# An edge pass of a graph kernel: a new begin of the pass, group words read earlier, a sorted stretch evicted at an earlier column, and per-group bookkeeping on VectorE

## The reference

```
n = x.shape[0]
h = x @ Wn + bn
for l in range(4):
    Q = h @ WQ[l] + bQ[l];  K = h @ WK[l] + bK[l];  V = h @ WV[l] + bV[l]
    scores = jnp.sum(Q[dst] * K[src], axis=-1) * scale
    e = jnp.exp(scores - segment_max(scores, dst)[dst])
    attn = e / segment_sum(e, dst, n)[dst]
    messages = segment_sum(attn[:, None] * V[src], dst, n)
    h = layernorm(h + messages @ WO[l] + bO[l], ln_g[l], ln_b[l])
return h @ Wout + bout
```

## Time and profile before

| what | value |
|---|---|
| time, median of 3 runs | 7103.49 us (7101.05 to 7110.28) |
| the profiled execution's own time | 7094.96 us |
| its span | 7093.5 us |
| busy: PE, PE's weight loads, DVE, ACT, POOL | 66%, 54%, 61%, 37%, 66% of the span |
| granted TensorE clock, mean | 0.811 |
| attend passes | about 798 to 1619, 1744 to 2566, 2690 to 3509, 3629 to 4448 us |
| heads pass | about 4763 to 5780 us |

### The profile page before, as it was taken

The page is one execution under the profiler, slowest core; times in us unless marked ns, Lnnn a source line. Parts: engine busy times, 40 slices in busy tenths (PEclk is TensorE's granted clock), DMA queues, the critical chain, the costliest instruction groups (busy, mean ns, idle before and its releaser), DMA issues. The chain is left out here.

```text
span 7093.5 us, 128253 instructions
## 1 busy us (share of the span) xinstructions
PE 4693.2 (66%) x28386; PEld 3840.8 (54%) x28387; DVE 4300.3 (61%) x13524; ACT 2623.5 (37%) x7476; POOL 4669.2 (66%) x4886
## 2 busy tenths in 40 slices
PE   5420377775777775777667777445555555998999
PEld 4310266654565554665546655323333334997998
DVE  7550266663666654666556666447776765776665
ACT  0200244434444443444444443315555543554111
POOL 1367577774777765777667777337777755776777
PEclk9555688887888887888778888677777776998999
DMA  5310233332333313333233333123333324333332
GB/s 188 99 37 0 62 92 91 88 84 63 87 90 89 89 50 96 89 90 89 62 86 89 89 90 82 49 89 105 105 105 105 105 69 117 97 96 84 96 95 82
DMA packets 404728, 615.56 MB, mean 87 GB/s; under 512 B 213510, under 2 KB 256049, under 8 KB 403940
## 3 DMA queue, kind: packets, MB, share of 16 engines
q0 software_dynamic: 169952, 363.29, 19.0%
q1 hardware_dynamic: 211190, 200.20, 9.9%
q10 hardware_dynamic: 23122, 47.29, 2.0%
HBM read 528.33 MB, written 82.09 MB: 86 GB/s over the span
## 5 line engine op out<-in xcount | busy, mean ns | idle before, releaser
L1973 POOL DMA_INDIRECT rows<-table_d,meta x2432 | 2307.4, 949 | 887.5 <-issue 728.6
L2037 PE MATMUL ps_total<-weighted_rows,ident 128*128 128x129 f32 (+1 forms) x6464 | 1404.3, 374 | 596.8 <-ACT weighted_rows L2197 483.7
L2037 PEld LDWEIGHTS ps_total<-weighted_rows,ident 128*128 128x128 f32 x6464 | 1149.8, 226 | 857.0 <-issue 670.4
L2373 DVE SCALAR_TENSOR_TENSOR prod<-rows,q_rows 128x129 f32<-128x129 f32 x2432 | 690.0, 293 | 639.3 <-issue 391.1
L1973 POOL DMA_INDIRECT rows<-pairs_d,meta x800 | 773.7, 967 | 257.7 <-issue 243.4
L2073 PE MATMUL dense_sums<-x_rows,dense_power_t 128*128 128x129 f32 x3528 | 593.9, 320 | 460.8 <-DVE dense_rows L2264 443.2
L2073 PEld LDWEIGHTS dense_sums<-x_rows,dense_power_t 128*128 128x128 f32 x3528 | 534.0, 230 | 501.5 <-issue 501.5
L2141 ACT ACTIVATE weighted_rows<-rows,power 128x129 f32<-128x129 f32 x2432 | 729.4, 389 | 5.1
L2159 ACT COPY dense_power_t<-dense_turned 128x512 f32<-128x512 f32 x504 | 265.1, 526 | 1030.7 <-PE dense_turned L2064 1022.1
L2197 ACT ACTIVATE weighted_rows<-once_weighted,of_relation 128x136 f32<-128x136 f32 x1600 | 485.6, 393 | 193.6 <-DVE once_weighted L2433 190.3
L2254 DVE CUSTOM_DVE_ANT_0 dense_masked<-dense_scores,dense_masked,dense_least 128x896 f32<-128x896 f32 x252 | 289.2, 1148 | 413.0 <-PE dense_scores L2055 289.9
(11 more groups left out here) (704 smaller groups left out, 8908.3 us busy)
## 6 DMA issues: line engine op xcount, KB each, us to landing
dense_masked<-dense_masks_d SPq DMA_DIRECT2D x252, 448.0 KB
rows<-table_d,meta POOLq DMA_INDIRECT x2432, 2.5
dense_masks_d<-unmasked ACTq DMA_DIRECT2D x9, 3136.0 KB
src_store<-near_window_d SPq DMA_DIRECT2D x50, 384.0 KB, 3.8
near_window<-near_window_d SPq DMA_DIRECT2D x48, 384.0 KB, 3.6
rows<-pairs_d,meta POOLq DMA_INDIRECT x800, 2.8
tile_rows<-table_d,tile_halves POOLq DMA_INDIRECT x441, 2.6
tile_rows<-made_d,tile_halves POOLq DMA_INDIRECT x441, 2.6
```

The lines of the kernel that those rows point to most:

```text
L1973: pool.indirect_dma_start(rows[q][:, j, 0:width], None, table_d, bass.IndirectOffsetOnAxis(meta[q][:, j, number:number + 1], 0)).then_inc( ...
L2037: mm = pe.matmul(total[:, q, ds(part, 1), 0:W].rearrange("p a w -> p (a w)"), k.ident[:], wide[:, j % WS, :], start=False, stop=True, skip ...
L2373: own(dve.scalar_tensor_tensor(prod[:, j % 2, :], rows[q][:, j, :], -1.0, query, ALU.mult, ALU.mult, accum_out=score[:, j, :]))
```

## The change

1. **Begin of a pass.** The constants stand outside a block, so the engines no longer meet behind them. ACT issues the load of `x_rows` only after the first list has landed (`listed[0]`), in parts of 8 and 41 tiles. PE turns the first two groups of tiles, then makes the queries and unit 0's scores, and then turns the other eleven groups, in other banks. ACT copies in that order. The nine loads of the next weights go from ACT's queue to SP's, behind the whole pass.
2. **Words read ahead.** In a dense turn PE calls `load_words` for group 0 after the first unit of the part (u = 0, u = 4). The clearing of the bank moves to `add_columns`.
3. **Sort's stretch** is evicted at step 0 (column 1) instead of step 5 (column 11). The wait for `placed` moves there from step 2.
4. **DVE's semaphores** `own` and `sorted` are cleared at the begin of a group or a turn, and count from 0.
5. **`step_of`** divides and takes the remainder.

```diff
+            def x_ps(n):
+                return dense_ps[:, n] if n < 2 else (sum_ps, power_ps)[n % 2]
...
-            return (loaded[j // PAIRS] >> ((6 if j < PAIRS else 0) + 2 * (j % PAIRS))) & 3
-
-        with nc.Block() as block:
-            @block.vector
-            def _(dve):
...
+            return loaded[j // PAIRS] // ((64 if j < PAIRS else 1) * 4 ** (j % PAIRS)) % 4
+
+        def constants_of_pass(dve):
...
+        constants_of_pass(nc.vector)
...
                     turns(sp, body)
+                    if fetch is not None:
+                        fetch_layer(sp, m, k, *fetch)
...
                         pe.sem_inc(read[q], 1)
-
+                        return loaded
+
+                    def clear_sums(i, q):
                         pe.wait_ge(m["sum_taken"], i * 2 + (q + 1))
                         clear(q)
-                        return loaded
 
                     def add_columns(i, q, loaded, columns):
+                        if columns[0] == 0:
+                            clear_sums(i, q)
...
                                 if u in (0, 4):
                                     count_earlier(i)
+                                    loaded = load_words(i, 0)
                                 if u == 2:
-                                    add_columns(i, 0, load_words(i, 0), range(S))
+                                    add_columns(i, 0, loaded, range(S))
                                 if u == UNITS - 1:
-                                    loaded = load_words(i, 0)
                                     add_columns(i, 0, loaded, range(S // 2))
...
-                        for n in range(XGROUPS):
-                            if n == 0 or n == 6:
-                                pe.wait_ge(m[f"x_loaded{n // 6}"], 16)
-                            if n >= 2:
-                                pe.wait_ge(m["xt"], n - 1)
+                        def turn_x(n):
                             for t in range(4 * n, min(4 * n + 4, T)):
-                                mm = pe.transpose(dense_ps[:, n % 2, ...], k.x1[:, t, 0:P], k.ident[:])
+                                mm = pe.transpose(x_ps(n)[:, ...], k.x1[:, t, 0:P], k.ident[:])
                             mm.then_inc(m["xt_ps"], 1)
-                        pe.wait_ge(m["xt"], XGROUPS)
+                        pe.wait_ge(m["x_loaded0"], 16)
+                        turn_x(0)
+                        turn_x(1)
+                        pe.wait_ge(m["xt"], 2)
                         turn_queries(0)
                         scores(0, 0)
+                        pe.wait_ge(m["x_loaded1"], 16)
+                        for n in range(2, XGROUPS):
+                            pe.wait_ge(m["xt"], n - 1)
+                            turn_x(n)
+                        pe.wait_ge(m["xt"], XGROUPS)
...
-                        for h, (t0, t1) in enumerate(((0, 24), (24, T))):
+                        act.wait_ge(listed[0], 48)
+                        for h, (t0, t1) in enumerate(((0, XFIRST), (XFIRST, T))):
...
-                    if fetch is not None:
-                        fetch_layer(act, m, k, *fetch)
...
-                        queries_over(0)
+                            if n == 1:
+                                queries_over(0)
...
                         if step == 0:
+                            dve.wait_ge(m["placed"], i + 1)
+                            dve.wait_ge(m["scattered"], i * 16 + 16)
+                            own(dve.tensor_copy(so.stretch[:], placed_ps))
+                            own(dve.scalar_tensor_tensor(so.idx[:], so.base[:], ...))
+                            own(dve.tensor_tensor(so.most[:], so.most[:], count_ps, ALU.max))
+                            own.wait()
+                            own(dve.scalar_tensor_tensor(so.base[:], count_ps, ...))
+                            dve.sem_inc(m["evicted"], 1)
...
                         for q in range(2):
-                            own = Steps(dve, m["own"], i * (2 * PER + 1) + q * PER)
+                            dve.sem_clear(m["own"])
+                            own = Steps(dve, m["own"])
...
+XFIRST = 8
```

75 lines of the change are left out of this document (36 added, 39 removed).

## The result

The changed kernel takes 7055.59 us, the median of four runs (7045.38 to 7061.28), against 7103.39 us for the kernel before on the same chip: a ratio of 0.993, with a 95% interval from 0.9916 to 0.9944. The forecast was 6950 us, with a range from 6920 to 7010. The sign was right and the size was not: 48 us came of 154. The profiled execution has a span of 7059.8 us at a granted TensorE clock of 0.801, against 7093.5 us at 0.811 before, so its difference is 33.7 us.

The account below looks back on a forecast made before the run. POOL's gathers were taken to bound the kernel. Boundaries 84, first turn 62, ends 7 and heads pass 1 made 154 us, from 7095 to 6941; with 8.5 us for the median, 6950 us, range 6920 to 7010.

Parts of the forecast that it names:

- POOL's pace of 1.25 us: Attend passes: each gather takes 0.949 us plus 0.30 us of issue on POOL, whatever the other engines do.
- Every other engine counts only where it makes POOL wait: Attend passes: POOL issues during 95% of a pass; others matter only by its waits, 147.7 us, or at the ends.
- theory V: From the experiments' expectations: VectorE's operations and the register instructions between them set the turns behind the first.
- The boundaries, 84 us: Every second boundary of turns: reading words earlier frees the list sooner and ends POOL's wait, 84 us, at most 98.
- still 4.1 us early [...] The whole wait goes: Turn boundaries: ACT's weighing frees the rows' buffer at 931.2 us, before POOL is ready at 935.3, so no wait remains.
- the boundaries stay, because another wait takes the place of PE's reading: Rival, turn boundaries: the rows' buffer or the list's landing makes POOL wait instead; 84 us missing, 7034 us, chance 0.07.
- The first turn, 62 us: Begin of each attend pass: earlier list and weighing start the second turn at about 837 us, gaining 15.5 us a pass.
- Registers, semaphores, the ends, 7 us: Fewer register instructions show only behind a pass's last gather, where PE ends 1.7 us sooner; 7 us in four passes.
- While POOL sets the pace this changes nothing: Turns: dropping three of four register instructions before a product on DVE, and partly on PE, has no effect there.
- a wait for finished work: DVE: clearing two semaphores a turn costs nothing, with 0.1 us each as upper bound.
- Division is slow: Rival, DVE columns and PE products: division costs the sequencer, deciding from 0.26 us a column; 7280 us, chance 0.03.
- What the profile would show: Signs: no stretch wait, one wait of about 5 us before the second turn, none later, 41.3 us turns, products 0.30 us apart.

Follow-up runs that it names:

- begin_and_words: The changed kernel with shift and mask, semaphores counted on, and eviction at the sort's sixth step taken back, leaving new begin and words read ahead: 6994.37 us.
- a_shift: The changed kernel with the step of a column taken by shift and mask again on both engines: 7002.78 us.
- b_words: The kernel before with only the words read ahead by TensorE: 7035.32 us.
- a_words_late: The changed kernel with TensorE reading a group's words where the kernel before does: 7108.33 us.
- begin_words_clears: The kernel with only new begin and words read ahead, plus the cleared VectorE semaphores: 7000.90 us.
- begin_words_early_evict: The kernel with only new begin and words read ahead, plus eviction at the sort's first step: 7000.65 us.
- begin_words_split: The kernel with only new begin and words read ahead, plus TensorE's sixteen first-group products split in halves around the next unit's scores: 6999.28 us.
- a_pe_shift: The changed kernel with shift and mask on TensorE alone, VectorE still dividing: 7024.05 us.
- a_dve_shift: The changed kernel with shift and mask on VectorE alone, TensorE still dividing: 7034.10 us.
- b_division: The kernel before with only division and remainder put in: 7124.20 us, ratio 1.0012.

## Why the prediction was wrong

**Where the 106 us went.** 154 us were forecast and 48 came. 66 us of the difference is what the three small parts cost together (begin_and_words against the change); the forecast had set them at nothing or at a gain. The other 40 us are the two large parts: the words brought 73 us of 84, and the new begin 41 us, where the first turn, the ends and the heads pass had been given 70 us. A part of those 70 is not in these two kernels: the early eviction shortens the first turn by another 3 to 4 us a pass.

**What bounds the kernel.** POOL's pace of 1.25 us was right: with begin and words alone the later turns take 41.6 us, 0.4 us above the 41.2 that the forecast comes to in this measure. "Every other engine counts only where it makes POOL wait" holds too. Wrong was to take from one execution, in which the late lists held all engines back together, that they would not make it wait. VectorE was nearly as full as POOL. Over two turns of the kernel before (85.5 us, mean over the four passes, counted over the trace's records of its operations and register instructions) it has gaps over 0.13 us of 5.5 us together and one of 2.9 us at the jump back of the loop, and for 77.1 us it or its sequencer works. POOL needs 82.6 us. In the change these are 86.0, 5.9, 3.2 and 76.9 us, in a_shift 84.3, 6.0, 3.3 and 75.0 us. The shift saves VectorE 1.9 us in two turns, and the pair of turns falls by 1.7 us. But its work is below POOL's in all of these; only with its gaps does VectorE's round get longer than POOL's. And the work alone does not order the kernels: begin_and_words has pairs of 83.5 us with 76.1 us of work and 7.4 us of gaps. So "VectorE's own stream" (theory V) is a part of the bound, not the whole.

**The boundaries, 84 us.** The mechanism was right and measures 73 us by itself (b_words). In the change only about 50 us of it came out (a_words_late), and new waits took the place of the old ones. The step that failed is "still 4.1 us early [...] The whole wait goes". The 4.1 us between ACT's weighing and POOL's need is a stock and not an income, and the forecast spent it itself. Its own first turn ends with a wait of about 5 us for the weighing (measured 4.42), so POOL begins the second turn with nothing to spare. The next two turns take 87.15 us from first gather to first gather (840.74 to 927.89), where POOL alone needs 82.6, and POOL waits for the weighing again, 3.93 us at the fourth turn. This second wait does not follow from the begin alone. In a_shift, with the same begin and the same eviction, POOL waits 4.86 us at the second turn and only 0.82 at the fourth; in begin_and_words no later wait for the weighing is over 0.3 us. The rival *the boundaries stay, because another wait takes the place of PE's reading* (7034 us, chance 0.07) describes the measured profile, and its time is the nearest of all. It gives no reason for the other wait, so the nearness is in part luck.

**The first turn, 62 us.** Right as a sum (58 us: the 60 us from the starts of the gathers, less 1.5 us that belong to the ends), with errors in it. The first gather comes at 794.94 us and not at 790.2: the list's last load, issued at 787.65 us, still takes 7 us. Two masks of 0.45 MB on SP's own queue follow it at once; whether they are the reason no run shows. So x_rows are issued at 794.02 us instead of 789.5, are there at 811.9 us (809 forecast), and the second unit is masked at 823.28 us (819.5). The weighing ends at 839.96 us (836.3 forecast), the second turn begins at 840.74 (837). From the last gather of a pass to the first of the next the gain is 9.9, 6.8 and 2.9 us. The wait for the stretch is gone, as forecast, but by the early eviction, which cost more than this in the turns behind.

**Registers, semaphores, the ends, 7 us.** This is where most was lost. "While POOL sets the pace this changes nothing" failed: with shift and mask back the kernel is 59 us faster, with the counting back 32 us. The clearing, "a wait for finished work" set at nothing, is a cost whose way is open. The ends themselves were worth 2 us and not 7: TensorE's last products end 12.65, 12.35, 12.55 and 12.60 us behind the last gather before, and 11.82, 12.42, 11.78 and 12.11 us in the change. In the first pass they take 5.55 us instead of 6.14, 0.35 us each, where 0.30 was forecast.

**Division is slow** (7280 us, chance 0.03) was the right mechanism at a small size. The division and remainder are one register instruction of 0.26 us on VectorE (the shift and mask took 0.07 + 0.045 us), just the point from which the rival was to decide. Its price was worked out as if beyond the spare nothing else gave way. In truth 24 ns a product are exposed on VectorE, and about half of the cost comes by way of TensorE, where I had seen none.

**The early eviction**, set at nothing behind the first turn, costs 0.3 to 0.5 us in each later turn. Its copies come ahead of the second mask in VectorE's order, and the 4.1 us that were to cover it were gone; that this order is the reason is argued, not shown.

**What the profile would show.** True: no idle time before the stretch, one wait of 4.42 us ended by the weighing before the second turn, no late lists at odd turns. Not true: no later waits, turns of 41.3 us. Half true: products of TensorE 0.30 us apart, which are 0.27 us at full clock and 0.35 us at the end of the first pass.

**The range.** Two of its margins are misadded. 84 less 70 us are 14 and not 20, and 98 less 84 us are 14 and not 8. With them right it reaches from 6914 to 7004 us, and the result lies outside all the same.

**A version that beats both.** begin_and_words takes 6994.37 us, 61 us less than the change. begin_words_clears, begin_words_early_evict, begin_words_split and a_shift lie within 9 us of it and are not told apart from it with certainty. Open is how TensorE's divisions cost time. In both pairs that differ by them alone the mean granted clock is lower with the division (0.801 and 0.820 for the change and a_pe_shift, 0.804 and 0.819 for a_dve_shift and a_shift). But the mean is a poor guide: begin_words_split (0.809) loses nothing without any division, and b_division (0.804) loses 8 us, and in both only 72 of the 512 scores run at the low level, as in every kernel with words read ahead and the shift on TensorE. In the kernels that divide on TensorE and read the words ahead, they are 104 to 143, and 100 in a_words_late. Whether the scores at the low clock make the loss was not tested by an edit.

## What to carry to other kernels

Time to spare between two engines at one boundary is not a rate. Before removing a wait, work out for each engine how long one round of the loop takes it, with register instructions, the loop's jump and its waits for other engines (here 86.0 us against POOL's 82.6, of which 76.9 us are work). If the forecast itself lets one engine wait for another at some point, nothing is left to spare between them from there on. An edit that costs little in one kernel (the division: 8 us in the kernel before) can cost much more beside another edit of the same change (50 us), so time the parts of a mixed change one by one. Register arithmetic of a column loop is part of the kernel, on VectorE and on TensorE.

## What the hardware showed that I had not expected

A register division with remainder takes 0.26 us on VectorE, against 0.07 + 0.045 us for shift and mask.

Where TensorE divides, a column's product took 0.27 us at full clock, and 0.38 us where it shifts and masks. This did not make the kernel faster: more of its scores ran at the low level of the granted clock, and these scores show what that costs. TensorE's rows in the third turn of the change's first pass, scores of the third unit and then of the fourth (idle time before in brackets):

```profile
908.48 0.22 PE L2014 MATMUL sort_made<-sort_totals,sort_earlier_bf 128*128 128x49 bf16 x1 [4.22 <-DVE sort_totals L2333]
911.31 2.08 PE L2062 MATMUL dense_scores<-sums,dense_asked_t 128*128 128x512 f32 x2 [2.61 <-DVE dense_least L2267]
...
918.31 1.03 PE L2062 MATMUL dense_scores<-sums,dense_asked_t 128*128 128x512 f32 x2
```

The windows over both, with PEclk as third column from the end:

```profile
908.00:911.00 3.00, 0.22 (x1) 0.10 (x1) 2.19 (x9) 0.00 (x0) 2.39 (x3) 0.50 0.21 56
911.00:914.00 3.00, 2.69 (x4) 1.35 (x5) 2.95 (x16) 1.59 (x3) 2.23 (x3) 0.50 0.16 45
918.00:922.00 4.00, 3.64 (x22) 2.40 (x20) 1.36 (x8) 0.91 (x2) 3.06 (x4) 1.00 0.64 174
```

At the level 0.50 (1.2 of 2.4 GHz) the two matmuls of 512 columns took 2.08 us, at 1.00 they took 1.03 us. The granted clock was still 1.00 from 900 to 904 us and 0.79 on the mean from 904 to 908; it fell in the 4.22 us in which TensorE was idle, and 2.61 us more without work followed behind one small matmul. These slow scores are what VectorE's third mask waits for until 914.98 us, ahead of the last step of the group at 918.43 us and of the weighing that POOL waits for.

The jump back of VectorE's loop, once in two turns, is a gap in its records: 2.7 to 3.6 us at the eight jumps of the first pass before, 3.2 to 4.0 us in the change. By the Trainium skill (Runtime: NRT & Kernel Launch, section Instruction fetch mechanics) a taken branch to instructions outside the loaded window makes the engine fetch them before it can go on. The trace agrees in that the gap stands behind each of these jumps; that it is a fetch, no run here shows.
